# Routing one-hot tables with the four choices innermost, four tiles per compare, row numbers multiplied in by ScalarE

## The reference, cut to what matters

```
logits = flat @ Wr.T + 0.5 * dom            # 2048 tokens x 64 experts
scores = softmax(logits)
_, topk_idx = top_k(logits + router_bias, 4)
topk_scores = scores at topk_idx, divided by their sum + 1e-8
out = sum over experts e of ((silu(flat @ Wg[e]) * (flat @ Wu[e])) * combine[:, e]) @ Wd[e]
out = out + shared experts
```

## Time and profile before

| | us |
|---|---|
| three runs of the kernel | 1088.12, 1077.11, 1088.92 |
| their median | 1088.12 |
| span of the profiled execution, first to last instruction | 1038.4 |
| mean granted TensorE clock in it, as a share of full speed | 0.889 |

### The profile page before, as it was taken

The page is one execution under the profiler, slowest core; times in us unless marked ns, Lnnn a source line. Parts: engine busy times, 40 slices in busy tenths (PEclk is TensorE's granted clock), DMA queues, the critical chain, the costliest instruction groups (busy, mean ns, idle before and its releaser), DMA issues. The chain is left out here.

```text
span 1038.4 us, 18942 instructions
## 1 busy us (share of the span) xinstructions
PE 845.1 (81%) x6846; PEld 712.1 (69%) x6846; DVE 754.9 (73%) x1679; ACT 384.4 (37%) x744; POOL 439.6 (42%) x582
## 2 busy tenths in 40 slices
PE   2899988898849865777888869999999986999973
PEld 2677777776638654666767648778878774887763
DVE  3668788886457793797656567888898755899994
ACT  2133343333323322333333344544555632434330
POOL 2023233323332305777776563666653220433332
PEclk9789999998679976999999965888888877999986
DMA  7000000000000034999998341211110000000001
GB/s 263 1 2 12 12 2 11 12 12 12 11 11 1 22 102 128 301 290 296 314 271 248 118 158 65 73 46 51 41 40 0 0 1 1 1 1 21 21 1 41
DMA packets 58299, 78.22 MB, mean 75 GB/s; under 512 B 9682, under 2 KB 50909, under 8 KB 58216
## 3 DMA queue, kind: packets, MB, share of 16 engines
q1 hardware_dynamic: 30952, 41.44, 12.7%
q0 software_dynamic: 9856, 18.92, 6.3%
q10 hardware_dynamic: 17408, 16.78, 4.7%
HBM read 62.40 MB, written 23.07 MB: 82 GB/s over the span
## 5 line engine op out<-in xcount | busy, mean ns | idle before, releaser
L497 POOL DMA_INDIRECT work<-xnd,rows_at x128 | 132.9, 1039 | 59.6 <-issue 32.3
L898 PE MATMUL ZO<-parts 128*128 128x256 f32 x288 | 92.5, 321 | 33.2 <-POOL parts L599 10.8
L455 POOL TENSOR_SCALAR_AFFINE_SELECT work<-work 128x256 f32<-128x256 f32 x128 | 53.4, 441 | 132.4 <-ACT work L628 132.4
L446 POOL TENSOR_SCALAR veps<-mv 128x2 f32<-128x2 f32 x64 | 17.5, 274 | 203.3 <-DVE mv L1434 203.0
L1841 DVE TENSOR_TENSOR work<-work,S 64x256 f32<-64x256 f32 x128 | 54.2, 424 | 59.8 <-ACT work L736 57.5
L628 ACT ACTIVATE work<-S 128x768 f32<-128x768 f32 x64 | 52.0, 812 | 105.9 <-PE S L969 105.9
L898 PEld LDWEIGHTS ZO<-parts 128*128 128x128 f32 x288 | 59.5, 207 | 41.6 <-issue 14.8
L899 PE MATMUL ZO<-parts 128*128 128x256 f32 x288 | 86.3, 300 | 0.0
L900 PE MATMUL ZO<-parts 128*128 128x256 f32 x288 | 86.0, 299 | 0.0
L599 POOL TENSOR_TENSOR parts<-work,parts 128x512 fp32r<-128x512 f32 x32 | 45.3, 1414 | 87.7 <-ACT parts L855 87.7
L898 PE MATMUL S<-xr,parts 128*128 128x512 f32 x192 | 79.2, 412 | 3.5 <-ACT work L843 2.7
(11 more groups left out here) (314 smaller groups left out, 2456.2 us busy)
## 6 DMA issues: line engine op xcount, KB each, us to landing
yd<-work ACTq DMA_DIRECT2D x64, 256.0 KB
raw<-in_experts SPq DMA_DIRECT2D x74, 192.0 KB
work<-in_experts SPq DMA_DIRECT2D x36, 192.0 KB
lg_all<-in_experts SPq DMA_DIRECT2D x18, 192.0 KB
raw<-in_ffn SPq DMA_DIRECT2D x2, 1536.0 KB, 7.2
x_sb<-in_x SPq DMA_DIRECT2D x1, 2048.0 KB, 8.5
xnd<-attn_w SPq DMA_DIRECT2D x8, 256.0 KB, 2.1
shd<-work SPq DMA_DIRECT2D x8, 256.0 KB, 2.3
```

The costliest lines, as they stand in the source:

```text
L455: last = pool.affine_select(out=diagonal, in_=diagonal, compare_op=ALU.is_ge, fill=0.0, base=0, pattern=[[0, 2], [1, P]], channel_multipli ...
L497: pool.indirect_dma_start(xg[:, i % RING, b, :], None, xnd[:], bass.IndirectOffsetOnAxis(ap=rows_at[:, 2 * i + b:2 * i + b + 1], axis=0), ...
L898: pe.matmul(dst, a(0), b(0), start=start, stop=False, skip_group_check=True)
```

## The change

`at_lo` and `at_hi` have the four choices innermost: for each tile, 128 x 4 values in place of 4 rows of 128. `iotah` holds each number four times (128 x 4) and is written just ahead of the routing in place of at the kernel's start. `row_hi` and `row_lo` become f16 (`row_sum` holds the f32 sum between). One DVE instruction compares a whole table of a round, four tiles x 128 x 4 = 2048 values per partition: two in a round, `at_hi` first, each raising `r_hot`. ACT multiplies the token numbers into `at_hi` in place, by tile, with `rowid` as a scale per partition (four instructions of 128x512 in a round, `token_marks`), and raises `r_oh`. PE waits for `r_oh` and for the second `r_hot` of the round, and reads each choice's 128 columns with a step of four values. Three semaphores of chained waits are gone, the chains go on with an existing one.

```
-        iotah = sb("iotah", [P, P], F16)
+        iotah = sb("iotah", [P, P, TOPK], F16)
...
-        row_hi = view([P, NT, TOPK])
-        row_lo = view([P, NT, TOPK])
-        at_lo, at_hi = ([view([P, 4 * TOPK, XB], F16) for _ in range(2)] for _ in range(2))
+        row_sum = view([P, NT, TOPK])
+        row_hi = view([P, NT, TOPK], F16)
+        row_lo = view([P, NT, TOPK], F16)
+        at_lo, at_hi = ([view([P, 4, XB * TOPK], F16).rearrange("p i (x k) -> p i x k", k=TOPK) for _ in range(2)]
+                        for _ in range(2))
...
+            def token_marks(c):
+
+                act.wait_ge(s["r_hot"], 2 * c + 1)
+                for i in range(4):
+                    last = act.activation(at_hi[c % 2][:, i].rearrange("p x k -> p (x k)"),
+                                          at_hi[c % 2][:, i].rearrange("p x k -> p (x k)"), ACT.Copy,
+                                          scale=rowid[:, 4 * c + i, 0:1])
+                last.then_inc(s["r_oh"], 1)
+
             for n in range(AHEAD):
                 hidden_unit(n)
                 if n == 5:
                     masks_by_tile()
                 if n in (6, 10):
                     shared_rows((n - 6) // 4)
+                if n == 10:
+                    token_marks(0)
+            for c in range(1, 4):
+                token_marks(c)
             shared_rows(2)
...
                 pe.wait_ge(s["r_oh"], c + 1)
+                pe.wait_ge(s["r_hot"], 2 * c + 2)
                 if c == 0:
                     pe.wait_ge(s["r_eb"], 1)
                 for j in range(4 * TOPK):
-                    last = pe.matmul(S[3][:, 0:XB], at_lo[c % 2][:, j, :], at_hi[c % 2][:, j, :],
+                    i, k = divmod(j, TOPK)
+                    last = pe.matmul(S[3][:, 0:XB], at_lo[c % 2][:, i, :, k], at_hi[c % 2][:, i, :, k],
                                      start=(c == 0 and j == 0), stop=(c == 3 and j == 4 * TOPK - 1))
...
-            dve.tensor_copy(iotah[:], iota[:])
...
-                chr_(dve.tensor_scalar(row_hi, top[:, :, 0:TOPK], 1.0 / P, 63.5 / P, ALU.mult, ALU.add))
-                chr_(dve.tensor_scalar(row_hi, row_hi, 8388608.0, None, ALU.add))
-                chr_(dve.tensor_scalar(row_hi, row_hi, -8388609.0, None, ALU.add))
+                chr_(dve.tensor_scalar(row_sum, top[:, :, 0:TOPK], 1.0 / P, 63.5 / P, ALU.mult, ALU.add))
+                chr_(dve.tensor_scalar(row_sum, row_sum, 8388608.0, None, ALU.add))
+                chr_(dve.tensor_scalar(row_hi, row_sum, -8388609.0, None, ALU.add))
...
-                for j in range(4 * TOPK):
-                    i, k = 4 * c + j // TOPK, j % TOPK
-                    dve.tensor_scalar(at_lo[c % 2][:, j, :], iotah[:], row_lo[:, i, k:k + 1], None, ALU.is_equal)
-                    last = dve.tensor_scalar(at_hi[c % 2][:, j, :], iotah[:], row_hi[:, i, k:k + 1], rowid[:, i, k:k + 1],
-                                             ALU.is_equal, ALU.mult)
-                last.then_inc(s["r_oh"], 1)
+                for at, row_part in ((at_hi, row_hi), (at_lo, row_lo)):
+                    last = dve.tensor_tensor(at[c % 2], bc(iotah[:].unsqueeze(1), [P, 4, XB, TOPK]),
+                                             bc(row_part[:, 4 * c:4 * c + 4, :].unsqueeze(2), [P, 4, XB, TOPK]),
+                                             ALU.is_equal)
+                    last.then_inc(s["r_hot"], 1)
...
             chr_(dve.tensor_copy(values16, bc(iota[:, 0:E].unsqueeze(2), [P, E, NT])))
+            dve.tensor_copy(iotah[:], bc(iota[:].unsqueeze(2), [P, P, TOPK]))
             task_softmax()
```

More of the change, by code:

```diff
@@ L301, in build @@
             a_wh a_wl a_xtl a_ztl a_yr a_xn2 a_x2t a_x2c a_xall a_xlo a_xm a_lg a_lgc
-            t_h1 t_h1c t_lg t_sub t_exp t_td t_tT t_tx t_dom r_sub r_exp r_mask r_tot r_used r_ebc r_ebT r_eb r_w
+            t_h1 t_h1c t_lg t_sub t_exp t_td t_tT t_tx t_dom r_sub r_exp r_hot r_mask r_tot r_used r_ebc r_ebT r_eb r_w
             f_g f_u f_sg f_h f_hh f_hl f_wh f_wl f_blk f_rows
@@ L308, in build @@
             d_g d_u d_sg d_h d_abs d_cmp d_hs d_hh d_hl d_dn d_x o_out
-            turn_t c_oe c_ol c_den chc0 cha chd chpc""".split()
+            turn_t c_oe c_ol c_den cha""".split()
         s = {n: sem(n) for n in names}
@@ L546, in head_event @@
                 pool.tensor_tensor(hv, hv, mhalf[:], ALU.pow).then_inc(s["c_hr"], 1)
-            cp = Chain(pool, s["chpc"])
             pool.wait_ge(s["r_w"], 1)
@@ L1825, in input_stats1 @@
                 ln_moments([tile(2 * b + t) for t in range(2)], ch)
-            ch = Chain(dve, s["chc0"])
             dve.wait_ge(s["x_st"], 16 * NB)
@@ L2024, in _ @@
             base += 4 * NB
-            ch = Chain(dve, s["chd"])
             def product(i):
```

## The result

The changed kernel took 1070.86 us (median of 4 runs, 1065.62 to 1074.34) beside 1088.52 for the kernel before (4 runs); the ratio is 0.9868 with a 95% interval of 0.9822 to 0.9915, so 1.3% faster (the two medians alone would give 0.984). Ratios here leave out executions that fell into a slower state of the chip. Five more rounds in another job gave medians of 1034.42 against 1045.47, ratio 0.9896 (0.9848 to 0.9943). The jobs stand at two levels, about 1088 and about 1045 us for the same kernel before, so only ratios within one job are compared.

A forecast was written before the change was run, and what follows sets the result against it. DVE's marking alone was taken to bound the table that starts the fixed-length expert stage; the new schedule ends L1721 at 381.7 instead of 394.73, so 1088.1 - 13.0 = 1075.1 us, range 1062 to 1083.

The forecast's parts named there:

- DVE alone bounds the table: Before the expert stage, DVE's 128 marking instructions set when `rows_at` is ready: some 27 us out of 29.9.
- A compare of 2048 f16 is 1.23 us: Each of 8 wide DVE compares of 2048 f16 values takes 1.23 us, judged from 1024 values taking 0.69.
- single values: Rival: DVE takes values singly in the wide compares, 2.3 us each; gain 7.4, time 1080.7 us; chance 0.14.
- a price for each row: Rival: DVE pays for each four-value row of a compare; at 10 ns a row, 1108 us; chance 0.06.
- Four multiplications on ACT 2.6 us: ACT's four 128x512 multiplications of a round take 2.6 us in a row, one alone 0.72.
- A batch at PE 1.6 us: PE's 16 products, operands at an 8-byte step, take 1.6 us at full clock: factor 1.5, bounds 1 and 2.
- The schedule: Marking stretch drawn step by step over DVE, ACT and PE: L1721 ends at 381.7 instead of 394.73, gain 13.0 us.
- The outlier that stood only in the range: One overlong DVE instruction, 1.1 us more or less, counted only in the forecast's own range of 1071 to 1078.
- ACT's multiplications lie on the loop four times (10.4 us): In the new loop of DVE, ACT and PE, ACT's four multiplications count four times, 10.4 us.
- The gain is passed on in full: The expert stage starts with the table, so all 13.0 us reach the end; rival, gain swallowed there: 1088, chance 0.07.
- A fixed length of 171.6 us for the gathers: POOL's 128 expert-stage gathers form a block of 171.6 us, 1.34 us each, that starts when the table is ready.
- The median lies 49.7 us over its span: The runs' median was read as 49.7 us above the profiled span of 1038.4, in time the change doesn't touch.

The follow-up runs named there:

- a_delay: Changed kernel plus 18 chained DVE instructions (13.1 us) that compute nothing, delaying the table `rows_at`; ratio to the kernel before 1.0023 (0.9986 to 1.0060).
- a_dve_mult: Changed kernel with ACT's 16 multiplications done by DVE instead; ratio to the kernel before 0.9881 (0.9844 to 0.9918), table ready 18.20 us after the block table's cast.
- b_act_multiplies: Kernel before, its 128 compares kept, with ACT multiplying the token numbers instead of DVE; table ready 31.97 us after the block table's cast, single time 1037.69 us.
- a_hi_contiguous: Changed kernel with the choices outside again in `at_hi` only, so PE's moving operand has no step; table 21.10 us after the block table's cast, single time 1035.39 us.
- a_again: Changed kernel unedited, five more rounds in another job; ratio to the kernel before 0.9896 (0.9848 to 0.9943), median 1034.42 us.
- a_pe_first: Changed kernel with PE's four batches ahead of the three down units of steps 9 to 11; ratio to the kernel before 0.9897 (0.9834 to 0.9960).

## Why the prediction was right, point by point

The forecast was a gain of 13.0 us and 1075.1; cast to table shows 12.5, and the medians of the first job differ by 17.7, while the ratio stands for 14.4 (9 to 19). The times alone couldn't tell 13 from 10 or 18; it is the traces and a_delay that show the mechanism.

- *DVE alone bounds the table.* Right. It held to 0.01 us over two profiles; fewer compares shorten it with all work still on DVE (a_dve_mult), and taking the multiplication away without fewer compares doesn't (b_act_multiplies).
- *A compare of 2048 f16 is 1.23 us.* Right: 1.21. Rows of four values cost nothing, and both rivals built on them (single values, a price for each row) are out. The price of single values was right too, 2.3 forecast, 2.28 measured where the innermost step is 0.
- *Four multiplications on ACT 2.6 us.* Right: 2.55.
- *A batch at PE 1.6 us.* Too low, the term that was mis-sized: 2.06, once for batch 1 and once for the last. It was worked out as a factor of 1.5 on the time at full clock; with the step the batch takes 2.05 at half clock too, so it is no factor on the clocked time. The chosen 1.5 lay between the contiguous row and the rows of a 32-byte step; the upper bound of 2 was nearly it (1.92). The rule of the Trainium skill that was weighed there (page "Advanced Engine Details and Errata", section "SBUF Cachelines": two reads from a 16-byte line give full speed) would have made it 1.07. For PE's moving operand the measurement contradicts it; for PE's weights (1.08 in a_hi_contiguous) it agrees, and for ACT's read nearly (2.67 against 2.55).
- *The schedule.* Counted from the cast, which was at 364.66 in the forecast: batch 1 starts at 9.5, measured 9.2; the last batch at 15.1, measured 15.1; table 17.0, measured 17.5. The difference is the last batch's 0.45 us; batch 1 was as much too short, but had started 0.4 sooner than drawn, so two small errors nearly cancel there. DVE, ACT and PE pass the round among themselves as drawn. The outlier that stood only in the range did come, 1.1 us in DVE's four compares of rounds 1 and 2 (5.74 us; 5.72, 5.73 and 5.69 in a_again, a_delay and a_pe_first). It cost next to nothing: it delays ACT's round 2, and round 3 waits for batch 1 and the compare behind it until that moment anyway.
- *ACT's multiplications lie on the loop four times (10.4 us).* Not by the prediction's own schedule: there round 3 waits for its compare behind batch 1 (377.1) and not for ACT's round 2 (376.75), so three lie on it, and the sum used three. In the trace the two come within 0.1 us of each other.
- *The gain is passed on in full.* Right: a_delay.
- *A fixed length of 171.6 us for the gathers.* True of the lower level: from the first start to the last 170.4 to 172.4 in eleven profiles (170.7 in the one that was read; its 171.6 ends about a microsecond later). Not of the upper one: 206.4, 206.3 and 207.5 in three.
- *The median lies 49.7 us over its span.* Wrong as a reading. 1.8 us lie around a span; the profile and the timed runs of before were of different levels. The forecast of the median survived since I took the gain from the profile and the level from the runs, and since the gain is, as far as the ratios tell, the same at either level; that was luck. The forecast of the span, 1025.4, did not.

## What to carry to other kernels

Many small compares against one table of numbers are worth turning into few wide ones if both operands keep a unit innermost step: 2048 f16 values in 1.21 us replaced 16 instructions at 0.19 us of pace each, even with the repeated operand in rows of four. Ask what the new layout costs the next reader, one operand at a time and at the clock it will have there, and let the engine in between turn it if that one reads it for little. And before a span is set against a median, look at the time of the profiled execution itself: levels that differ by 4% between jobs hide an effect of 1%, a stretch between two named instructions doesn't.

## What the runs showed that was not expected

- PE's moving operand of 128 f16 values at a step of 8 bytes: 16 products in 2.06 us against 1.07 contiguous at full clock, and 2.05 against 1.87 to 1.90 at half; at the same step PE's weight load and ACT's read cost 0.0 and 0.03 us an instruction.
- Single DVE instructions take 0.2 to 1.1 us too long. In four kernels whose DVE stream is the same up to there, the group with the outlier is as long within 0.05 us; in other kernels the outliers lie elsewhere. What causes them was not tried.
- At the upper level POOL's gathers stretch from 171 to 207 us with waits for PE and for an unnamed source. The later jobs at the lower level ran on chips 13 and 7, the one at the upper level on chip 4; whether the chip is the cause was not tried and stays open.
